# A transformer layer on one core: feed-forward down products in plain fp32, and another opening on GpSimd

## What the reference computes

```
xn   = layernorm(x)
attn = softmax(rope(q) rope(k)^T / sqrt(8)) v @ Wout + bout      # 16 heads of 8 channels
w    = top-2 of sigmoid(xn @ gate_w + gate_b), divided by their sum
e(h) = (silu(xn @ wg) * (xn @ wu)) @ wd                          # 64 hidden channels
out  = x + attn + xn + e_shared + sum over 16 experts of w * e_expert
```

## Time and profile before

| | |
|---|---|
| median of 3 runs | 245.02 us (244.97 to 245.06) |
| the profiled execution | 243.89 us, its span 242.1 us |
| busy: TensorE, its weight loads | 211.7 (87%), 140.2 us |
| busy: VectorE, GpSimd, ScalarE | 189.4 (78%), 173.8 (72%), 139.6 us (58%) |
| chain that ended last | TensorE 58%, VectorE 15%, GpSimd 15%, issue 5%, DMA 3%, ScalarE 2% |
| `hid_lo` on GpSimd, L1136 | 36 times, 46.2 us |
| `hid_hi` on ScalarE, L775 | 33 times, 20.8 us |
| down product L385 to L387, 128 rows | 32 times three, 483, 396 and 394 ns each |

### The profile page before, as it was taken

One profiled execution on the slowest core, in us unless ns is written; L12 is line 12 of the kernel. 1 busy time (PEld: TensorE's weight loads), 2 busy tenths in 40 slices (PEclk: granted clock), 3 DMA queues, 4 the chain that ended last, 5 costly groups with the idle time before them and its releaser, 6 DMA issues.

```text
span 242.1 us, 4855 instructions
## 1 busy us (share of the span) xinstructions
PE 211.7 (87%) x1612; PEld 140.2 (58%) x1612; DVE 189.4 (78%) x407; ACT 139.6 (58%) x262; POOL 173.8 (72%) x254
## 2 busy tenths in 40 slices
PE   0484948588998999999998999999999999999993
PEld 0353624355565666676675567666766657676652
DVE  5897966699988787999975878998688878876521
ACT  2475122233766756665566676666676767676662
POOL 9195699899964749987848487879886775548722
PEclk9998897999999999999999999999999999999998
DMA  7924454621260554320674241406523641212101
GB/s 225 367 56 128 124 160 137 185 51 40 62 189 3 153 163 126 94 59 10 194 207 125 67 136 40 114 5 178 154 68 107 201 145 35 90 20 73 45 3 43
DMA packets 35953, 26.53 MB, mean 110 GB/s; under 512 B 4236, under 2 KB 30156, under 8 KB 35916
## 3 DMA queue, kind: packets, MB, share of 16 engines
q1 hardware_dynamic: 35224, 25.30, 35.5%
q10 hardware_dynamic: 704, 0.92, 1.0%
HBM read 18.53 MB, written 7.47 MB: 107 GB/s over the span
## 4 chain that ended last, share of the span: by engine, by line
PE 58%; DVE 15%; POOL 15%; issue 5%; DMA 3%; ACT 2%; SPq 0%; POOLq 0%; DVEq 0%; ACTq 0%
PE PV L546 10%; PE S2b L527 5%; PE S2a L527 4%; PE S1a L507 4%; PE S1b L507 4%; POOL hid_lo L1136 3%; DVE mx L1001 3%; PE Y L385 3%; PE FB L385 3%; POOL gu L1120 3%; PE FA L385 3%; PE FA L386 3%; PE FA L387 3%; PE FB L387 3%; PE FB L386 3%
## 5 line engine op out<-in xcount | busy, mean ns | idle before, releaser
L1136 POOL TENSOR_TENSOR hid_lo<-gu,hid_hi 128x512 fp32r<-128x512 f32 (+1 forms) x36 | 46.2, 1282 | 25.1 <-ACT hid_hi L775 23.3
L732 ACT ACTIVATE probs<-S2b 128x512 f32<-128x512 f32 x62 | 37.0, 597 | 28.2 <-PE S2b L527 28.0
L1001 DVE TENSOR_REDUCE mx<-S1b 128x2 f32<-128x512 f32 x63 | 43.1, 683 | 10.7 <-PE S1b L507 10.6
L1001 DVE TENSOR_REDUCE mx<-S1a 128x2 f32<-128x512 f32 x65 | 44.4, 683 | 5.5 <-PE S1a L507 5.5
L732 ACT ACTIVATE probs<-S2a 128x512 f32<-128x512 f32 x62 | 37.1, 599 | 14.2 <-PE S2a L527 12.1
L1120 POOL TENSOR_TENSOR gu<-gu,wbc 128x512 f32<-128x512 f32 x32 | 40.9, 1279 | 6.0 <-DVE gu L988 6.0
L546 PE MATMUL PV<-probs,vx 128*32 128x256 f32 x512 | 35.0, 384 | 0.4 <-ACT probs L732 0.4
L775 ACT ACTIVATE hid_hi<-gu 128x512 fp32r<-128x512 f32 (+1 forms) x33 | 20.8, 631 | 21.2 <-POOL gu L1120 19.4
L1010 DVE SCALAR_TENSOR_TENSOR th<-th,FA 128x512 f32<-128x512 f32 (+1 forms) x36 | 24.6, 682 | 10.7 <-ACT th L744 9.9
L744 ACT ACTIVATE th<-FA 128x512 f32<-128x512 f32 (+1 forms) x36 | 21.5, 596 | 14.2 <-PE FA L387 13.9
L507 PE MATMUL S1a<-k_hat,q_hat 96*128 96x256 bf16 x130 | 25.3, 276 | 1.2 <-DVE mx L1001 1.0
(11 more groups left out here) (181 smaller groups left out, 441.4 us busy)
## 6 DMA issues: line engine op xcount, KB each, us to landing
wbc<-route_w SPq DMA_DIRECT2D x64, 128.0 KB, 3.0
q_hat<-q_parts SPq DMA_DIRECT2D x32, 96.0 KB, 2.6
k_hat<-k_parts SPq DMA_DIRECT2D x32, 96.0 KB, 2.6
k_parts<-parts SPq DMA_DIRECT2D x8, 192.0 KB, 2.1
q_parts<-parts SPq DMA_DIRECT2D x8, 192.0 KB, 2.2
x_sb<-in_x SPq DMA_DIRECT2D x4, 256.0 KB, 4.1
q_parts<-parts SPq DMA_DIRECT2D x8, 128.0 KB, 2.1
k_parts<-parts SPq DMA_DIRECT2D x8, 128.0 KB, 2.1
```

Source lines behind the costliest of these rows:

```text
L732: nc.scalar.activation(probs[:, head % (2 * NQ), :], exp_bank(head)[:], ACT.Exp, scale=SCALE).then_inc(exp_done, 1)
L1001: nc.vector.tensor_reduce(mx[:, (q // QB) % 2, (q // 2) % 2, :, q % 2, i], S1[use % 2][:].rearrange("p (t s) -> p t s", t=SB), axis=AX.X, ...
L1136: nc.gpsimd.tensor_tensor(hid_lo[0:rows, m % 2, :], gu[0:rows, m % 2, :], hid_hi[0:rows, m % 2, :].bitcast(f32), ALU.subtract).then_inc(hi ...
```

## The change

1. Down products become one plain fp32 matmul of `wd_sb` with the weighted `gu`. `hid_hi`, `hid_lo`, `wd_hi`, `wd_lo` and all that makes them go. `wd_sb` gets its own tensor.
2. `gu` has three buffers. The multiplication of chunk m waits for the down product of chunk m - 3.
3. GpSimd: `xT_lo` of group 1 stands behind the wait for batch 0's parts; three splits of group 1 move in the block table; batch 0's residual sum goes from block 1 to block 0.
4. The spare rotary products use two banks: two in block -5, two in block -4, read by VectorE in blocks -5 and -3.
5. The router weights of group 0 are written to DRAM by SyncE, not ScalarE.
6. For groups 2 and 3 ScalarE copies bank FA into `xT` first and rounds `xT_hi` from `xT`.

```diff
+GU_SLOTS = 3
-    (1, 0, 0): -5, (1, 0, 1): -3, (1, 1, 0): -4, (1, 1, 1): -1,
+    (1, 0, 0): -5, (1, 1, 0): -3, (1, 0, 1): -1, (1, 1, 1): 1,
-RESIDUAL_BLOCK = (1, 8, 22, 23)
+RESIDUAL_BLOCK = (0, 8, 22, 23)
-        wd_hi, wd_lo = sb("wd_hi", [P, NCH, C], f32r), sb("wd_lo", [P, NCH, C], f32r)
+        wd_sb = sb("wd_sb", [P, NCH, C])
-        ROPE_BANK = (S2[1], PV, S2[0], Y)
+        ROPE_BANK = (S2[1], PV)
...
@@ SyncE, behind load_hats(1) @@
+            sp.wait_ge(fb_read, B_USE["G6", 0] + 1)
+            sp.dma_start(w_dram[0].rearrange("e (b t) -> b e t", t=P), wT[:]).then_inc(wd_done, 16)
@@ TensorE, down(n) @@
-                pe.wait_ge(hid_ready, n + 1)
-                if n < NCH:
-                    pe.wait_ge(down_split, n + 1)
...
-                split_product(Y[:], wd_hi[0:rows, c, :], wd_lo[0:rows, c, :], hid_hi[0:rows, n % 2, :],
-                              hid_lo[0:rows, n % 2, :], c == 0, c == NCH - 1).then_inc(down_done, 1)
+                pe.wait_ge(gu_weighted, n + 1)
+                nc.tensor.matmul(Y[:], wd_sb[0:rows, c, :], gu[0:rows, n % GU_SLOTS, :],
+                                 start=c == 0, stop=c == NCH - 1).then_inc(down_done, 1)
@@ TensorE, block loop @@
-                    if i == 0 and n == 1:
-                        for at in range(4):
-                            spare_rope(at)
+                    if (i == 0 and n == 1) or (i == 2 and n == 2):
+                        for half in range(2):
+                            spare_rope(2 * (n - 1) + half)
@@ ScalarE, read_a of G1 @@
+                        nc.scalar.activation(xT[:, gp, :], FA[:], ACT.Copy).then_inc(fa_read, 1)
+                        act.wait_ge(fa_read, A_USE[kind, g] + 1)
+                        nc.scalar.activation(xT_hi[:, gp, :], xT[:, gp, :], ACT.Copy).then_inc(xhi_ready, 1)
@@ VectorE @@
-                        if m >= 2:
-                            dve.wait_ge(hid_ready, m - 1)
+                        if m >= GU_SLOTS:
+                            dve.wait_ge(down_done, m - GU_SLOTS + 1)
-                    if i == 3 and n == 1:
-                        for w in range(2):
-                            read_spare_rope(w)
+                    if i == 3 and n in (1, 3):
+                        read_spare_rope(n // 2)
@@ GpSimd @@
-            xt_low(1)
             pool.wait_ge(parts_done[0], 2 * PARTS)
+            xt_low(1)
...
-                if 0 <= m < NCH:
-                    down_low(m)
-                if 0 <= m < NCHUNKS:
-                    rows = I if m % NCH == 0 else P
-                    pool.wait_ge(hid_hi_ready, m + 1)
-                    nc.gpsimd.tensor_tensor(hid_lo[0:rows, m % 2, :], gu[0:rows, m % 2, :],
-                                            hid_hi[0:rows, m % 2, :].bitcast(f32), ALU.subtract).then_inc(hid_ready, 1)
```

More of the change, by code:

```diff
@@ L196, in layer_kernel @@
         th = sb("th", [P, 2, GT])
-        gu = sb("gu", [P, 2, GT])
-        hid_hi, hid_lo = sb("hid_hi", [P, 2, GT], f32r), sb("hid_lo", [P, 2, GT], f32r)
+        gu = sb("gu", [P, GU_SLOTS, GT])
         yT = sb("yT", [P, 2, GT])
@@ L517, in exp_scores @@
                         pe.wait_ge(ld_kones, 32)
+                        pe.wait_ge(spare_v_read, 1)
                         pe.wait_ge(spare_rope_read, 4)
@@ L570, in down @@
                 rows = I if c == 0 else P
-                pe.wait_ge(hid_ready, n + 1)
-                if n < NCH:
-                    pe.wait_ge(down_split, n + 1)
+                if n == 0:
+                    pe.wait_ge(ld_down, 32)
                 if c == 0:
@@ L687, in read_b @@
                     nc.scalar.activation(wT[:], FB[0:NTB * E, 0:P], ACT.Copy).then_inc(fb_read, 1)
-                    act.wait_ge(fb_read, B_USE[kind, g] + 1)
-                    act.dma_start(w_dram[g].rearrange("e (b t) -> b e t", t=P), wT[:]).then_inc(wd_done, 16)
+                    if g:
+                        act.wait_ge(fb_read, B_USE[kind, g] + 1)
+                        act.dma_start(w_dram[g].rearrange("e (b t) -> b e t", t=P), wT[:]).then_inc(wd_done, 16)
                 elif kind == "T2":
@@ L768, in _ @@
                         nc.scalar.activation(vx[:, 0, :, 1, :, 2 * D:3 * D], v[:, :, :, 1, :], ACT.Copy).then_inc(spare_v_read, 1)
-                    if i == 2 and 0 <= n - 1 < LAST_ROUNDINGS:
-                        rows = I if (n - 1) % NCH == 0 else P
-                        act.wait_ge(gu_weighted, n)
-                        if n >= 3:
-                            act.wait_ge(down_done, n - 2)
-                        nc.scalar.activation(hid_hi[0:rows, (n - 1) % 2, :], gu[0:rows, (n - 1) % 2, :],
-                                             ACT.Copy).then_inc(hid_hi_ready, 1)
                     if i == 3 and 0 <= n - 2 < NCHUNKS and (n - 2) % NCH == NCH - 1:
@@ L881, in read_spare_rope @@
                     dve.wait_ge(spare_rope_ready, at + 1)
-                    nc.vector.scalar_tensor_tensor(rope[:, w, half, :], ROPE_BANK[at][:], bias_sb[:, at:at + 1],
+                    nc.vector.scalar_tensor_tensor(rope[:, w, half, :], ROPE_BANK[half][:], bias_sb[:, at:at + 1],
                                                    (cos_sb, sin_sb)[half][:], ALU.add, ALU.mult).then_inc(spare_rope_read, 1)
@@ L985, in _ @@
                         dve.wait_ge(fa_read, A_USE["hg", m] + 1)
-                        if m >= 2:
-                            dve.wait_ge(hid_ready, m - 1)
-                        nc.vector.tensor_tensor(gu[0:rows, m % 2, :], FB[0:rows, :], th[0:rows, m % 2, :],
+                        if m >= GU_SLOTS:
+                            dve.wait_ge(down_done, m - GU_SLOTS + 1)
+                        nc.vector.tensor_tensor(gu[0:rows, m % GU_SLOTS, :], FB[0:rows, :], th[0:rows, m % 2, :],
                                                 ALU.mult).then_inc(fb_read, 1)
@@ L1022, in _ @@
                             read_b(kind, g)
-                    if i == 2 and LAST_ROUNDINGS <= n - 1 < NCHUNKS:
-                        round_hidden(n - 1)
                     for g, stage in route_stages(blk, i):
@@ L1090, in xt_low @@
                 else:
-                    pool.wait_ge(fa_read, A_USE["G1", g] + 1)
+                    pool.wait_ge(xhi_ready, g)
                 nc.gpsimd.tensor_tensor(xT_lo[:, g % 2, :], xT[:, g % 2, :], xT_hi[:, g % 2, :].bitcast(f32),
                                         ALU.subtract).then_inc(xlo_ready, 1)
-            def down_low(c):
-                rows = I if c == 0 else P
-                if c == 0:
-                    pool.wait_ge(down_hi_ready, 1)
-                nc.gpsimd.tensor_tensor(wd_lo[0:rows, c, :], wd_sb[0:rows, c, :], wd_hi[0:rows, c, :].bitcast(f32),
-                                        ALU.subtract).then_inc(down_split, 1)
+            pool.wait_ge(parts_done[0], 2 * PARTS)
             xt_low(1)
-            pool.wait_ge(parts_done[0], 2 * PARTS)
             for w in range(2):
@@ L1119, in _ @@
                         pool.wait_ge(wbc_ld[c - 1], 32 * (g + 1))
-                        nc.gpsimd.tensor_tensor(gu[:, m % 2, :], gu[:, m % 2, :], wbc[:, g % 2, c - 1, :],
+                        nc.gpsimd.tensor_tensor(gu[:, m % GU_SLOTS, :], gu[:, m % GU_SLOTS, :], wbc[:, g % 2, c - 1, :],
                                                 ALU.mult).then_inc(gu_weighted, 1)
@@ L1124, in _ @@
                         xt_low(g)
-                for g in range(G):
+                for g in range(1, G):
                     if blk == RESIDUAL_BLOCK[g]:
@@ L1128, in _ @@
                 for (g, w, slot), at in SPLIT_BLOCK.items():
-                    if blk == at:
+                    if blk == at and g > 1:
                         split_batch(w, g, slot)
-                if 0 <= m < NCH:
-                    down_low(m)
-                if 0 <= m < NCHUNKS:
-                    rows = I if m % NCH == 0 else P
-                    pool.wait_ge(hid_hi_ready, m + 1)
-                    nc.gpsimd.tensor_tensor(hid_lo[0:rows, m % 2, :], gu[0:rows, m % 2, :],
-                                            hid_hi[0:rows, m % 2, :].bitcast(f32), ALU.subtract).then_inc(hid_ready, 1)
+                for (g, w, slot), at in SPLIT_BLOCK.items():
+                    if blk == at and g == 1:
+                        split_batch(w, g, slot)
+                if blk == RESIDUAL_BLOCK[0]:
+                    residual(0)
                 for kind, g in early_b(blk):
```

27 lines of the change are left out of this document (8 added, 19 removed).

## The result

The kernel after takes 240.72 us (median of 4 runs, 240.37 to 241.54), the kernel before 245.00 us (4 runs, 244.72 to 245.06): a ratio of 0.9843 with a 95% interval of 0.9811 to 0.9875. The forecast was 242.1 us in a range of 237.8 to 245.2. The profiled execution took 240.37 us, its span is 238.2 us; the forecast for it was 241.0.

What follows compares the result with a forecast made beforehand. TensorE's matmuls were taken to bound the kernel from chunk 6 on, a chain through GpSimd before. Opening -5.5, product +4.6 and slack -2.0 gave -2.9: 241.0 us profiled, 242.1 us median, 8-in-10 range 237.8 to 245.2.

Steps and rivals of the forecast that it cites:

- The product's term: TensorE from chunk 6 on: a plain fp32 down product costs +0.15 us each, 31 products, +4.6 us.
- The rival with exposed weight loads: TensorE's down products: each fp32 record exposes its weight load, 1.02 us a product, 247.1 us; chance 0.06.
- the one with four equal passes: TensorE's down products: four passes at an fp32r record's length, 0.94 us a product, 244.9 us, no change; chance 0.06.
- The full part's slack: From chunk 6's to the last multiplication on VectorE: TensorE's waits shrink by 2.0 of 5 us, bounds 0 and -4.
- The opening's term: Up to chunk 6's multiplication on VectorE: it starts at 55.9 against 61.38, -5.5 us, bounds -7.5 and -3.
- Chunk 0: First multiplication on VectorE: moving `xT_lo` ends a slow `rest` subtraction sooner, net gain 0.8 us.
- Chunk 1: Its multiplication on VectorE: 0.8 us from `xT_lo` and 1.3 us from two rotary reads off VectorE, 31.22 to 29.1.
- Chunk 2: Its multiplication: six VectorE steps, 3.6 us, plus 1.4 for rotary products and router's projection on TensorE, at 34.1.
- The DMA that is late next: Chunk 3's `wbc` loads on SyncE start at about 41.4, land at 45.0 and cost chunk 5 1.0 us.
- The reasons given for the opening: Before chunk 6: 0.8 us from moving `xT_lo`, 1.3 us from two rotary reads, GpSimd's 1.64 us less a block.
- The rival in which the opening gives more and the slack returns: Opening -7.5 without the DMA in the way, slack -3.5, product +4.6: 238.6 us; chance 0.20.
- The change doing nothing: Whole kernel: no effect, for instance because GpSimd's removed work was never waited for; chance 0.03.

Runs made afterwards that it cites:

- the kernel with three fp32r products: After with each down product as three fp32r matmuls of the same rounded values, low parts left out: 236.67 us, 0.9615 to 0.9685 of before.
- GpSimd load: After with one more unread 128x512 fp32 GpSimd subtraction a block from block 1 on: 242.86 us, 0.9900 to 0.9953 of before.
- the two traces at full clock: After with group 1's `xT_lo` back ahead of batch 0's parts (241.07 us), and after with three fp32r matmuls a down product (236.67 us).
- The old order: Before with only the plain fp32 down products and three value buffers, all engines' order as before: 242.45 us, 0.9867 to 0.9941 of before.
- the order alone: After's new order with the three fp32r down products, `hid_hi`, `hid_lo`, `wd_hi` and `wd_lo` kept: 246.34 us, 1.0026 to 1.0090 of before.
- the early loads: After with SyncE loading router weights of chunks 3 and 4 ahead of the hats of batches 2 and 3: 240.68 us, 0.9788 to 0.9857 of before.

## Why the prediction was right, point by point

The mechanism held: TensorE pays for the dearer product in the full part, and the opening and the slack give back more. The size held less well. The medians fell by 4.3 us where 2.9 were forecast, and two of the three terms were off by 2.0 and 0.9 us with opposite signs, so it is partly luck that the sum is nearer than the larger of its terms.

- **The product's term** was right in rate and in size. 0.853 us was worked out, 0.86 is on the timeline; +4.6 us was forecast, 4.59 measured by the kernel with three fp32r products. The rival with exposed weight loads (1.02 us) and the one with four equal passes (0.94 us) are both excluded by the row at 100.17. The count of four passes in the Trainium skill (FP8 and Floating Point Precision, "TensorE Precision Notes") fits only if a pass is shorter than an fp32r matmul of this kernel: 0.86 / 4 = 0.215 us against 0.235.
- **The full part's slack** was mis-sized: -2.0 was taken out of an estimated 5, with bounds of 0 and -4. It is -4.0 (166.99 to 163.01), on the bound, so the stretch is 167.6 us and not 169.6. I had read one 1386 ns instruction and one 0.9 us wait, and counted them. The wait for `xT` is worth 0.25 us; GpSimd's load is worth 2.0, twice what I gave it. The rule of the Trainium skill (SBUF — State Buffer, "Who interferes with whom"), that such instructions exclude each other, agrees with VectorE's 4.0 us more in the GpSimd load's row. The -2.0 that I took by it was still only half of what came back, and no run tells an exclusion from a shared bandwidth by the size of the slack.
- **The opening's term** was -5.5 forecast and -4.6 measured, inside its bounds. Chunk 0 was half right: the `rest` subtractions take 0.4 us twice and the gate product of chunk 0 starts 0.85 us sooner (21.64; 22.49), but its multiplication only 0.41 us sooner, where 0.8 was forecast. Between them a cast of the router takes 0.67 us in place of 0.17 while a GpSimd split runs. Chunk 1 was forecast at 29.1 and came at 29.84. Of this 0.4 us is the gain missing at chunk 0, and 0.27 is a wait for the up product. The router's transpose and the up product start 0.4 us sooner than before (28.84), but the up product's three matmuls follow each other 0.33 and 0.41 us apart, before 0.33 and 0.24: the clock had fallen (0.69 between 28 and 30 us).

```profile
27.80 0.27 PE L468 MATMUL FB<-ident_sb,wtok 128*64 128x128 f32 x1 [1.45 <-DVE gu L974]
28.43 0.52 PE L384 MATMUL FB<-xT_hi,wu_hi 128*128 128x512 f32 x1 [0.36 <-ACT wT L689]
28.76 0.61 PE L385 MATMUL FB<-xT_hi,wu_lo 128*128 128x512 f32 x1
```

- Chunk 2 was forecast at 34.1, 5.0 us after chunk 1, and came 6.45 us after it. In the two traces at full clock the step is 5.23 and 5.09 us. So the step through VectorE and TensorE was right to 0.2 us; the other 1.2 us I put down to the lower level of the clock, which the forecast had nowhere. Each of these traces also has an edit of its own.
- **The DMA that is late next** was named rightly and mis-sized: forecast to start at 41.4 and land at 45.0, it starts at 42.39 and GpSimd goes on at 46.17. The loads were to move 1.5 us forward, because the weights leave 0.8 us sooner and by SyncE. The first ones moved 0.4 us (30.54; 30.94): the store is issued 0.41 us sooner (28.40; 28.81) and its loads follow 2.14 us after it from SyncE, 2.13 from ScalarE, so the change of the issuing engine gave nothing. Chunk 5 came at 51.04 (forecast 50.1), and chunk 6 follows 5.73 us later (forecast 5.75), so the 0.9 us that the opening's term missed were there at chunk 5. At most 0.47 of them, GpSimd's wait, is the DMA itself; GpSimd's own work ended at 45.70, and no run says what would have brought that forward.
- **The reasons given for the opening** were wrong in part. I put 0.8 us on the place of `xT_lo` and carried it through to the loads, and 1.3 us on the two rotary reads, which the forecast gives back at chunk 3. The old order reaches chunk 6 at 56.50 without either, in a trace with a higher clock. They show where they are made (chunk 0 by 0.66 us for the first, chunk 1 by 1.1 for both) and are gone at chunk 5. What did shorten the opening is what the old order drops too: GpSimd's 1.64 us a block, and ScalarE's rounding ahead of the tanh, which I had left out and which costs 0.7 to 1.2 us at chunk 6 when it is put back into after. With the order alone chunk 6 stays at 62.27. No run drops one of the two and keeps the other.
- The third buffer was counted at nothing and is worth nothing. GpSimd's busy time was forecast at 124 and is 125.1 us.
- The rival in which the opening gives more and the slack returns (238.6 us) had the slack right (-3.5; -4.0) and the opening wrong (-7.5). The change doing nothing is excluded by after's ratio and by the old order's.

The errors were -2.0 us in the slack, +0.9 in the opening and +0.1 behind, in sum -1.0 on the span (forecast 239.2, which is 242.1 less 2.9; measured 238.2). The execution is 0.6 us under its forecast of 241.0, as 0.4 us more of it lies outside the span.

## What to carry to other kernels

A split product costs more than its matmuls: here the plain one cost TensorE 4.6 us more in the full part, and with the split's makers gone 4.6 us of opening and 4.0 us of slack came back. To size slack on the engine that bounds a stretch, run that engine's work with the disputed work of the others left out, and compare the stretches; the waits that I could name one by one gave half. A saving ahead of a DMA that is awaited is worth nothing until the DMA moves, so step a forecast through to the next fixed landing, and carry only what is left there. Compare an edit of a few tenths of a us only with a trace whose clock went the same way: the early loads gave nothing beside one trace and 0.54 us beside another.
